# A four-layer network on one core: layer 2's readout in two passes, layer 0's row scalings on ScalarE, and a new order of all steps of layers 0 to 2

## The reference

```python
# layer 0, mixer (state space, per head h of 4, 64 wide; the kernel takes tiles of 128 tokens)
xdt = x * dt                                  # row scaling
Y_diag = (C B^T * exp(segsum(A dt))) @ xdt
states = B^T @ (decay_states * xdt)           # row scaling
new_state = exp(A_total) * old_state + states
# layer 2, mixer, after a recurrence over the tokens (S: two states of 16 for each of 16 heads)
y = retrieved.reshape(b, l, 32) @ readout_w   # 32 -> 256
mean, var = over (tokens, 16 channels) for each of 16 groups and each sequence
y = ((y - mean) * rsqrt(var + eps)) * gn_w + gn_b
y = y * silu(z) + D_param * x_conv
s = x + y @ out_w
# layer 2, feed-forward: 8 experts of 176, top 2, in bf16
h = square(relu(x_e @ w_up)); out += h @ w_down
```

## Time and profile before

| | us |
|---|---|
| median of 3 runs | 3108.1 (3099.51 to 3109.42) |
| profiled execution, its own time | 3114.71 |
| its span | 3110.6 |
| VectorE busy | 2533.6 (81%) |
| TensorE busy | 2417.1 (78%) |
| ScalarE busy | 1623.2 (52%) |
| GpSimd busy | 573.1 (18%) |

### The profile page before, as it was taken

How to read it: one execution, slowest core, us unless ns; L and a number is a source line. 1 busy time by engine, 2 the same in 40 slices (tenths; PEclk the granted TensorE clock), 3 DMA queues, 4 the chain that set the end, 5 groups by cost and what they waited for, 6 DMA issues and landing times.

```text
span 3110.6 us, 40132 instructions
## 1 busy us (share of the span) xinstructions
PE 2417.1 (78%) x13729; PEld 1316.2 (42%) x13729; DVE 2533.6 (81%) x5554; ACT 1623.2 (52%) x3180; POOL 573.1 (18%) x610
## 2 busy tenths in 40 slices
PE   3687886867967958868758576685799889889988
PEld 1333333333333433333433132222466667666763
DVE  4387798998998999999988978967587778777864
ACT  1334535335245245344353355544688778778862
POOL 0000300400401203004003003003232223323320
PEclk9798987887978978978878678887799999999999
DMA  2001110101101111101011011032778887888750
GB/s 76 0 17 50 26 31 24 31 27 31 34 26 29 31 35 24 32 21 29 26 52 40 26 41 27 1 108 75 224 236 232 228 219 222 232 221 234 228 171 27
DMA packets 271861, 267.89 MB, mean 86 GB/s; under 512 B 15336, under 2 KB 244218, under 8 KB 270122
## 3 DMA queue, kind: packets, MB, share of 16 engines
q1 hardware_dynamic: 271658, 265.33, 29.8%
HBM read 132.51 MB, written 124.39 MB: 83 GB/s over the span
## 4 chain that ended last, share of the span: by engine, by line
DVE 39%; PE 34%; ACT 14%; issue 9%; DMA 1%; POOL 1%; SPq 1%; DVEq 0%; POOLq 0%; ACTq 0%
PE banks L2735 6%; PE banks L2781 3%; PE banks L2695 2%; DVE t L1018 2%; ACT t L2722 2%; DVE t L1170 2%; DVE t L953 2%; ACT t L2646 2%; PE banks L2637 1%; DVE t L2711 1%; ACT L145 1%; ACT xT L1396 1%; DVE t L808 1%; DVE t L809 1%; ACT t L512 1%
## 5 line engine op out<-in xcount | busy, mean ns | idle before, releaser
L2711 DVE CUSTOM_DVE_ANT_0 t<-banks,t 128x640 f32<-128x640 f32 (+7 forms) x512 | 379.8, 751 | 102.8 <-POOL t L2680 39.1
L2722 ACT ACTIVATE t<-t 128x640 f32<-128x640 f32 (+7 forms) x512 | 389.9, 779 | 58.2 <-DVE t L2711 56.9
L2735 PE MATMUL banks<-ident,t 128*128 128x128 f32 x2304 | 364.6, 283 | 46.4 <-ACT t L2722 26.8
L2735 PEld LDWEIGHTS banks<-ident,t 128*128 128x128 f32 x2304 | 253.9, 143 | 122.0 <-ACT t L2722 54.2
L2676 POOL TENSOR_TENSOR t<-t 128x512 f32<-128x512 f32 x96 | 122.7, 1278 | 536.6 <-DMA t<-relative_scratch 482.7
L549 POOL TENSOR_TENSOR t<-t 128x512 f32<-128x512 f32 x28 | 48.1, 1719 | 914.7 <-ACT t L521 914.7
L2695 PE MATMUL banks<-t 128*128 128x512 bf16 (+3 forms) x768 | 204.2, 335 | 9.6 <-DVE t L2711 9.1
L2766 DVE COPY t<-banks 128x512 f32<-128x512 f32 x256 | 176.1, 688 | 37.1 <-PE banks L2735 33.5
L1086 PE MATMUL banks<-t 128*128 128x512 f32 x256 | 144.1, 646 | 40.2 <-DVE t L1166 30.5
L1120 ACT ACTIVATE t<-banks 128x512 f32<-128x512 f32 x128 | 76.5, 597 | 188.0 <-PE banks L1086 187.9
L1090 PE MATMUL banks<-t 128*128 128x512 f32 x256 | 141.6, 636 | 13.2 <-DVE t L1170 12.7
(11 more groups left out here) (454 smaller groups left out, 6012.0 us busy)
## 6 DMA issues: line engine op xcount, KB each, us to landing
relative_scratch<-t SPq DMA_DIRECT2D x128, 512.0 KB, 3.4
t<-relative_scratch SPq DMA_DIRECT2D x128, 512.0 KB, 5.3
relative_scratch<-t SPq DMA_DIRECT2D x128, 256.0 KB, 4.1
t<-in_wmoe SPq DMA_DIRECT2D x64, 384.0 KB, 3.1
t<-cut_scratch SPq DMA_DIRECT2D x192, 64.0 KB
xT<-xT SPq DMA_DIRECT2D x16, 512.0 KB, 4.2
cut_scratch<-t SPq DMA_DIRECT2D x8, 768.0 KB, 4.1
z_scratch<-t SPq DMA_DIRECT2D x8, 512.0 KB, 3.0
```

The costliest lines, as they stand in the source:

```text
L2711: nc.vector.tensor_tensor_reduce(s.s[z][:, 0:n], ps[:, b0:b0 + 1 + i // 4, :].rearrange("p b n -> p (b n)")[:, 0:n], s.bias[r][:, j, WIDE ...
L2722: nc.scalar.activation(s.s[z][:, 0:n], s.s[z][:, 0:n], ACT.Exp, scale=-1.0, bias=s.least[:, z:z + 1]).then_inc(*a.mark("weights", u))
L2735: nc.tensor.transpose(ps[:, 4 + c % 2, (t - lo) * P:(t - lo + 1) * P], s.s[u % NS][:, t * P:(t + 1) * P], k.ident[:]).then_inc(*e.mark("tu ...
```

## The change

- The mixer's row scalings move from VectorE to ScalarE as four copies with a scale each, one per head: xdt straight behind btok, xdd and (units 1 to 7) the decayed state, into a new tile `kept`, behind the decays. TensorE's y waits for xdd from ScalarE and low from VectorE; VectorE's sum onto the state waits for kept. The tile's VectorE steps fall from six to four, ScalarE's rise from three to six.
- The readout sums its input over the tokens (two reductions), gets all means from that, makes one pass of matmuls and squares over all four batches, one root for all, and then a second pass of the same matmuls, with ScalarE's copy doing the scaling and shifting out of the bank. y gets a second buffer (in `pairs`), z and x_conv three buffers of half a batch each, loaded in eight parts; the third buffer lies over the x ring and `restart`, so its load waits for the stores of x.
- The two squares per expert of layer 2 become one of 128x1024; the unused rows are cleared once.
- The strings of PE, ACT, DVE and SP are all written anew; POOL's stays. Counted from the strings (before, after): letters of DVE 3282, 3132, of ACT 1465, 1554, of PE 1619, 1630. Pairs "rr" in DVE's 757, 848. n and o behind the last b in PE's 68, 76; n and o behind the last r in DVE's 76 (four to an expert), 72 (three to an expert). p in PE's 33, 44. Behind the gated decay (L611) of a tile the next letter in units 2 to 7 is now r for the last three tiles, and f or a for the first.

In the diff the readout's old functions are left out (they stand above).

```diff
-MIXER, HEADS, EXPERTS, STRAND = 12496, 7168, 5772, 4224
+MIXER, HEADS, EXPERTS, STRAND = 12752, 7168, 5772, 4224
...
-            pe.wait_ge(v, "xdd", u, t)
-            pe.wait_ge(a, "btok", u, t)
+            pe.wait_ge(v, "gated_low", u, t)
+            pe.wait_ge(a, "xdd", u, t)
             mm(o, s.xdt[:, h, :], s.low[:, h, :], start=True, stop=first).then_inc(*e.mark())
...
-        act.wait_ge(v, "xdt", u, t)
+        act.wait_ge(e, "turned", u, t)
         nc.scalar.copy(s.btok[:], ps[:, 0, DI0:DI0 + P]).then_inc(*a.mark("btok", u, t))
+        yield
+        for h in range(H0):
+            nc.scalar.activation(s.xdt[:, h, :], ps[:, 0, h * HP:(h + 1) * HP], ACT.Copy, scale=s.dt[:, t, h:h + 1]).then_inc(
+                *a.mark("xdt", u, t))
         yield
         act.wait_ge(v, "low", u, t)
...
         nc.scalar.activation(s.dd[:], s.dd[:], ACT.Exp).then_inc(*a.mark("decay", u, t))
+        yield
+        act.wait_ge(a)
+        for h in range(H0):
+            nc.scalar.activation(s.xdd[:, h, :], s.xdt[:, h, :], ACT.Copy, scale=s.dd[:, h:h + 1]).then_inc(*a.mark("xdd", u, t))
+        if u:
+            yield
+            if t:
+                act.wait_ge(v, "state", u, t - 1)
+            for h in range(H0):
+                nc.scalar.activation(s.kept[:, h, :], s.state[:, t, h, :], ACT.Copy, scale=s.ec[:, h, P - 1:P]).then_inc(
+                    *a.mark("kept", u, t))
...
-        dve.wait_ge(e, "turned", u, t)
-        tt(s.xdt[:], ps[:, 0, 0:DI0].rearrange("p (h q) -> p h q", h=H0), rep(s.dt[:, t, :], 2, HP), ALU.mult).then_inc(*v.mark("xdt", u, t))
...
         dve.wait_ge(a, "decay", u, t)
-        tt(s.low, s.low, rep(s.gm[:], 1, H0), ALU.mult).then_inc(*v.mark())
-        tt(s.xdd[:], s.xdt[:], rep(s.dd[:], 2, HP), ALU.mult).then_inc(*v.mark("xdd", u, t))
+        tt(s.low, s.low, rep(s.gm[:], 1, H0), ALU.mult).then_inc(*v.mark("gated_low", u, t))
...
-            tt(s.state[:, t], s.state[:, t], rep(s.ec[:, :, P - 1], 2, HP), ALU.mult).then_inc(*v.mark())
-            yield
-            dve.wait_ge(v)
-            tt(s.state[:, t], s.state[:, t], new, ALU.add).then_inc(*v.mark("state", u, t))
+            dve.wait_ge(a, "kept", u, t)
...
 TURNS_PE = (
...
+    "agbtfpneiommmmfmmmmmmfffffffffmmffmmmmmmfffmmmmmmmmmmmmmmmmmmmmmmeememaeaamaafeemeeemeeemeeeeeeefeeeeeffmeeffeff"
...
 TURNS_DVE = (
...
+    "aafafeamaeafaemrrramafeamafafeffefafafefmfrfefefmffafrfrfrfafmfefrfaeerarabmreriarerbrbrmrmrerrrrraraarrrrrmrrrr"
+    "rrrrrrrrrrrirrrirmrrrrrrrrrrrrrrirrrmmiiiriririrrrmrrrrrrrrrrrrrrrrrrrrmrrrrrrrrrrrmrmrrrrrrrrrrrrrrrrrrrrrrrirr"
+    "rrrrrrrrrrrrrrrrrrirrmrrrrirrrmrigimiigigggggmggggggggggggggmgmmmferrrmraeaeaeaeaeaeaeaeaaeaeafameamafaeafafaeea"
...
-        s.xdt, s.xdd, s.btok = take((H0, HP)), take((H0, HP)), take((P,))
+        s.xdt, s.xdd, s.kept, s.btok = take((H0, HP)), take((H0, HP)), take((H0, HP)), take((P,))
...
-        s.x = [sb([P, TB]) for _ in range(RINGX)]
+        spare = sb([P, RINGX * TB + SCAN])
+        s.x, s.restart = [spare[:, n * TB:(n + 1) * TB] for n in range(RINGX)], spare[:, RINGX * TB:]
...
-    o.sums, o.stat, o.ab = first((2, 2)), first((2, 2)), first((2, 2))
+    o.part, o.rsum, o.ysum, o.shift, o.scale = first((2, B)), first((B,)), first((2, B)), first((2, B)), first((2, B))
+    o.sums, o.var, o.nm = first((2 * B, 2)), first((2, B)), first((2, B))
...
-    o.y = second((2, T))
-    o.zx, o.sq = third((4, T)).rearrange("p (w j) t -> p w j t", w=2), third((TB,))
+    o.y = [second((2, T)), s.pairs[:].rearrange("p (j t) -> p j t", j=2)]
+    o.zx = [third((2, T)), third((2, T)), spare[:].rearrange("p (w t) -> p w t", w=2)]
+    o.sq = third((TB,))
...
-    def zx_back(b):
-        for j in range(2):
-            sp.dma_start(chunks(s.zx[:, 0, j]), of_batch(keep.z[:, j], b)).then_inc(*z.mark(b))
-            sp.dma_start(chunks(s.zx[:, 1, j]), of_batch(keep.xconv[:, j], b)).then_inc(*xc.mark(b))
+    def zx_back(n):
+        b, j = divmod(n, 2)
+        sp.dma_start(chunks(s.zx[n % 3][:, 0]), of_batch(keep.z[:, j], b)).then_inc(*z[n % 3].mark(n))
+        sp.dma_start(chunks(s.zx[n % 3][:, 1]), of_batch(keep.xconv[:, j], b)).then_inc(*xc[n % 3].mark(n))
...
+    zx_back(1)
+    yield
     k.sp.wait_ge(k.line("in2_dve"), "kq", LAST)
     k.sp.wait_ge(k.line("turn2_act"), LAST, 1, 3)
     xn_back(5)
     xn_back(7)
     yield
+    for n in range(RINGX):
+        k.sp.wait_ge(k.queue(f"x1_stored{n}"), LAST - (LAST - n) % RINGX)
+    zx_back(2)
+    yield
...
-    for b in range(1, B):
-        yield
-        k.sp.wait_ge(v, "y", b - 1)
-        zx_back(b)
+    for n in range(3, 2 * B):
+        yield
+        k.sp.wait_ge(v, "y", n - 3)
...
+    nc.vector.memset(s.half[0].hid[:, 1], 0.0).then_inc(*v.mark())
...
+def readout2_pe(k, s):
     nc, pe, ps, (e, a, v) = k.nc, k.pe, k.ps, readout2_lines(k)
     mm = nc.tensor.matmul
+
+    def out(b, h):
+        for j in range(2):
+            mm(bank(ps, S0 + h), s.out_w[:, j], s.y[b % 2][:, j, h * TB:(h + 1) * TB], start=(j == 0), stop=(j == 1)).then_inc(
+                *e.mark("out", b, h))
+
+    yield
+    pe.wait_ge(v, "rsum")
+    pe.wait_ge(k.queue("o2_reads"), "all")
+    for j in range(2):
+        mm(ps[:, S0 + 1, j * B:(j + 1) * B], s.read_w[:, j * P:(j + 1) * P], s.rsum[0:2 * NH], start=True, stop=True).then_inc(*e.mark("ysum"))
+    yield
+    pe.wait_ge(v, "ysum")
+    mm(ps[:, S0, 0:2 * B], s.group, s.ysum.rearrange("p j b -> p (j b)"), start=True, stop=True).then_inc(*e.mark("mean"))
+    for b, j, h in BJH:
+        yield
+        n = 4 * b + 2 * j + h
+        if n < 2:
+            pe.wait_ge(v, "mean")
         else:
+            pe.wait_ge(a, "square", n - 2)
+        mm(bank(ps, S0 + h), s.read_w[:, j * P:(j + 1) * P], s.ret[:, b, h * TB:h * TB + TB], start=True, stop=True).then_inc(
+            *e.mark("first", n))
+    yield
+    pe.wait_ge(v, "sums")
+    mm(ps[:, S0, 0:2 * B], s.group, s.var.rearrange("p j b -> p (j b)"), start=True, stop=True).then_inc(*e.mark("var"))
+    for b in range(B + 1):
+        if b < B:
+            for j in range(2):
+                for h in range(2):
+                    yield
+                    if j:
+                        pe.wait_ge(a, "y", b, 0, h)
+                    elif b >= 2:
+                        pe.wait_ge(v, "summed", b - 2, h)
+                    elif b:
+                        pe.wait_ge(a, "y", 0, 1, h)
+                    else:
+                        pe.wait_ge(a, "root")
+                    mm(bank(ps, S0 + h), s.read_w[:, j * P:(j + 1) * P], s.ret[:, b, h * TB:h * TB + TB], start=True, stop=True).then_inc(
+                        *e.mark("second", b, j, h))
+        if b:
+            for h in range(2):
+                yield
+                pe.wait_ge(v, "y", 2 * b - 1)
+                if b < B:
+                    pe.wait_ge(a, "y", b, 1, h)
+                else:
+                    pe.wait_ge(v, "summed", B - 2, h)
+                out(b - 1, h)
+
+
+BJH = [(b, j, h) for b in range(B) for j in range(2) for h in range(2)]
+
+
+def readout2_act(k, s):
     nc, act, ps, (e, a, v) = k.nc, k.act, k.ps, readout2_lines(k)
+    for b, j, h in BJH:
+        n = 4 * b + 2 * j + h
+        yield
+        act.wait_ge(e, "first", n)
+        act.wait_ge(v, "mean")
+        if n:
+            act.wait_ge(a)
+        nc.scalar.activation(s.sq, bank(ps, S0 + h), ACT.Square, bias=s.nm[:, j, b:b + 1],
+                             accum_out=s.sums[:, j * B + b, h:h + 1]).then_inc(*a.mark("square", n))
     yield
     k.table(ROOT)
+    act.wait_ge(e, "var")
+    nc.scalar.activation(s.scale.rearrange("p j b -> p (j b)"), ps[:, S0, 0:2 * B], ACT.Sqrt, bias=k.eps5[:]).then_inc(*a.mark("root"))
+    for b, j, h in BJH:
+        yield
+        act.wait_ge(e, "second", b, j, h)
+        act.wait_ge(v, "shift")
+        if b >= 2:
+            act.wait_ge(e, "out", b - 2, 1)
+        nc.scalar.activation(s.y[b % 2][:, j, h * TB:(h + 1) * TB], bank(ps, S0 + h), ACT.Identity, scale=s.scale[:, j, b:b + 1],
+                             bias=s.shift[:, j, b:b + 1]).then_inc(*a.mark("y", b, j, h))
+
+
+def readout2_dve(k, s):
     nc, dve, ps, (e, a, v) = k.nc, k.dve, k.ps, readout2_lines(k)
     tt = nc.vector.tensor_tensor
     yield
+    dve.wait_ge(k.queue("ret_back"), "all")
+    nc.vector.tensor_reduce(s.part[0:2 * NH, 0], s.ret[:, :, 0:LAST * P], AX, ALU.add).then_inc(*v.mark())
+    yield
+    dve.wait_ge(k.line("back_act"), "out", LAST)
+    nc.vector.tensor_reduce(s.part[0:2 * NH, 1], s.ret[:, :, LAST * P:], AX, ALU.add).then_inc(*v.mark())
+    yield
+    dve.wait_ge(v)
+    tt(s.rsum[0:2 * NH], s.part[0:2 * NH, 0], s.part[0:2 * NH, 1], ALU.add).then_inc(*v.mark("rsum"))
+    yield
+    dve.wait_ge(e, "ysum")
+    nc.vector.tensor_copy(s.ysum.rearrange("p j b -> p (j b)"), ps[:, S0 + 1, 0:2 * B]).then_inc(*v.mark("ysum"))
+    yield
+    dve.wait_ge(e, "mean")
```

(48 more changed lines are left out.)

210 lines of the change are left out of this document (64 added, 146 removed).

## The result

The kernel after takes 3148.6 us (median of 4 runs, 3140.2 to 3153.6), the kernel before beside it 3108.8: ratio 1.0121, 95% interval 1.0101 to 1.0142. It is slower by 1.2%, where the forecast was 3075 and the range ended at 3118. The profiled execution took 3153.6 us.

A forecast was written before the change was run, and what follows sets the result against it. VectorE was taken as the bound, busy 202.62 of 215.2 us per repeating unit. Terms -31 -3 +9 -3 -4 gave -32 us, the readout -1: 3082 us profiled, 3075 as a median, range 3050 to 3098.

The forecast's parts named there:

- Scalings to ScalarE, -31: Mixer: moving 92 row scalings off VectorE, 0.34 us each, saves 31.3 us, taken whole.
- Copies in the queue, 0: ScalarE's queue before L1741: the new copies cost nothing; other end 12 us per unit.
- Stall with GpSimd, 0: L612's stall beside GpSimd's L549 passes to the next instructions, so 0 gained; other end 31 us.
- Waits in the new order, "unchanged": VectorE's waits stay 12.6 us per unit; ends 6 us per unit either way, 36 us over six units.
- Pairs of r, +9: VectorE's string: 91 more pairs of neighbouring dependent recurrence steps at 0.10 us each cost 9 us.
- work moved, -4: Two layer 2 experts more behind the recurrence take 4 us of VectorE work from before it.
- Squares, -3: Layer 2's experts: one merged square instead of two saves 0.07 us for each of 48 experts, 3 us.
- readout, -1: Stretch behind the recurrence: two-pass readout, TensorE 113 us plus 8 us tail, 121 against 122 us.
- As denser work could make it: Readout stretch: TensorE's clock nearer 1.0 (0.95) would gain 17 us; at 0.70, 17 us lost.
- Rival 3: Slower: ScalarE's copies get in the recurrence's way before L1741, about 1 us per group; 3134 us, chance 0.17.
- Rival 2: Nothing comes of it: bound leaves VectorE, mixer's chain sets the unit, TensorE fills the readout; 3105 us, chance 0.13.

The follow-up runs named there:

- copies-later kernel: Kernel before with all three row scalings as ScalarE copies, from unit 2 on one to three steps later in ScalarE's order: 3108.5 us, ratio 1.0006.
- copies-later kernel with the padding: Kernel before with the row scalings as later-placed ScalarE copies, plus readout products zero-padded from 32 to 128 partitions: 3112.6 us, ratio 1.0032.
- scalings-only: Kernel before with only the mixer's three row scalings moved from VectorE to ScalarE, in the order of before: 3126.8 us, ratio 1.0075.

## Why the prediction was wrong, step by step

**Scalings to ScalarE, -31: the step that failed.** "I take this whole, since VectorE is the bound wherever the mixer runs" took a busy share of 94% for a bound. The work did leave (202.6 to 198.3 us), at the price worked out. But with the copies late the unit is 215.0 us, what it is with all 202.6. In nine kernels in the old order (before among them) the three repeating units take 645.1 to 645.3 us together, in two 655.6 and 655.7, and never between; VectorE's work only changes its gaps. In the new order 11 us by medians, 20 by ratios, were gained, of the 31.

The traces do show what the unit keeps step with: TensorE's granted clock. In the copies-later kernel the clock falls 128.8 us behind each unit's mark (770.7, 985.7 and 1200.8) and rises 27.3 us later:

```profile
899.60:926.80 27.20, 13.28 (x54) 8.31 (x54) 26.45 (x43) 13.03 (x42) 3.54 (x2) 0.50 0.04 11
1114.60:1141.80 27.20, 13.26 (x55) 8.30 (x54) 26.45 (x42) 12.98 (x42) 3.54 (x2) 0.50 0.04 10
```

It does so in all three units to within 0.02 us, and at the same place in the copies-later kernel with the padding, another execution. In the kernel before it falls 126.9, 123.4 and 126.9 us behind the marks, so there the repetition is less exact. A unit that repeats in step with the clock would keep its length when VectorE's work shrinks by a few us. That the clock does the holding isn't shown: no run changed the clock inside the unit.

**Copies in the queue, 0: failed.** L1741's 44.8 us of waiting were read as slack. It waits for VectorE and is wanted at once when VectorE has answered, so a copy that starts in that pause can still delay it. In the old order it is 18 to 21 us, shown by moving the copies' places alone. The prediction looked at L1705 only; the experts' activation made VectorE wait 9.8 us in three units, L1705's wait grew by 8.5. Since the unit has only been seen at two lengths in this order, 3.5 us a unit isn't the price of so many copies.

**Stall with GpSimd, 0: right, or nearly.** In the old order VectorE's work fell by 4.3 us a unit; with the stall gone as well it would have been 4.1 and four times 1.07, 8.4. In the new order a step of the recurrence stands behind L623 (before L611) and takes the stall over:

```profile
1175.81 0.69 DVE L623 TENSOR_TENSOR t<-t 128x512 f32<-128x512 f32 x1
1175.85 1.77 POOL L564 TENSOR_TENSOR t<-t 128x512 f32<-128x512 f32 x1 [16.41 <-ACT t L525]
...
1176.42 0.22 DVE L1707 TENSOR_REDUCE t<-t 128x4 f32<-128x68 f32 x1
1176.67 1.04 DVE L1710 TENSOR_TENSOR t<-t 128x64 f32<-128x64 f32 x1
1177.74 0.24 DVE L1714 TENSOR_REDUCE t<-t 128x16 f32<-128x80 f32 x1
...
1178.54 0.26 DVE L1710 TENSOR_TENSOR t<-t 128x64 f32<-128x64 f32 x1
```

L1710, with two SBUF inputs, takes 1.04 us instead of 0.26 beside GpSimd's L564 (before L549), while the reduction ahead of it, with one, keeps its 0.22. L623, which had begun 0.04 us ahead of L564, keeps its 0.69. By the rule of the Trainium skill (GPSIMD Engine Reference, Key points) it is the two SBUF inputs that count; for the instructions that began beside L564 the trace agrees.

**Waits in the new order, "unchanged": failed,** and past the bad end of its bounds (6 us a unit either way). Gaps were 12.6 us a unit and are 18 to 25, 7.7 more on average; three units give 23 us more of them, less 4 of work, which is the 19.3 lost. In the unit cut above they lie at both ends. That these gaps come from the order's places for ScalarE's steps is read from the waits; no run tested it.

**Table loads: not counted.** They follow from ScalarE's string and can be counted before any run: 90 before, 142 after. The excess cost 8 to 13 us, not clear of the noise.

**Pairs of r, +9, and work moved, -4.** The dropped mixer steps account for 30 of the 91 new pairs (787 in the scalings-only string), the merged squares for 31 (788), the new order for the other 30. For the experts moved behind the recurrence the prediction went by TensorE's string, which says two; VectorE's says five (76 steps of four to an expert, 72 of three), 9 us at the prediction's own 1.8 us each. No run has the price of either term by itself.

**Squares, -3, and readout, -1.** The 0.25 us by which the projection waits longer was named, for the stretch behind the recurrence, and then left out of the sum; in the old order the kernel with the merged squares is 15 us slower, in the new one they cost nothing. TensorE after the recurrence was to be busy 113 us in 121; it was 116 in 131.6. The term was short by 9 us, inside the 17 given for a lower clock. "As denser work could make it" went the wrong way round: in the densest 41 us the clock stood at 0.50.

**Rivals.** Rival 3 (0.17) had the right sign and, in the old order, the right mechanism; its 3134 was 15 us short. It doesn't describe the new order, where L1714 waits only 3.1 us. Rival 2's first words, "the bound leaves VectorE", are what the copies-later run showed, at 3108.5 us against its 3105; the mixer's chain, which it named in VectorE's place, wasn't shown to be what holds the unit. **Open:** whether the granted clock pins the unit at 215.0 us; why parts that cost 21, 15 and 21 us alone, 57 in sum, cost 46 together; what the new order does to the code of before, which was never run in it; and how much of the 6 us in layer 3 is chance (its part took 952 to 973 us over these kernels).

## What to carry to other kernels

An engine that is busy 94% with an order written out by hand isn't yet the bound: move a small piece of its work away and look whether the period moves, before summing up what it saves. If the period doesn't move, see whether something else repeats with it, such as the granted clock. When work goes to an engine that "waits anyway", ask who waits for that engine and how soon; put the new instructions behind the answers, not ahead of them. A stretch on TensorE that never pauses can still run at half its clock; look at the granted clock there before doubling such products.

## What the runs showed of the hardware

In a stretch of 41 us in which TensorE was busy 40.53 us, most of it (38 of 54 products) over 32 partitions, the granted clock was 0.50; with the same products filled with zero rows to 128 partitions it was 0.92, and the stretch behind the recurrence was 13 us shorter in either order. The Trainium skill (TensorE: Matmul & The Clock Gate, Part 1) has the clock double under sustained matmul work; the stretch without the padding disagrees, the padded one agrees. Where other products stand between them, as in the kernel before, padding took the stretch from 123.6 to 117.0 us. And the repeating unit took 215.0 us in nine kernels of the old order and 218.6 in two, with VectorE's work in it anywhere from 198.3 to 202.7 us, and in the copies-later kernel the granted clock fell and rose at the same places of each unit.
